# The first factor of a block inverse: from a product with the identity to a transposition on VectorE, with new weights and ranks for the list scheduler

## The reference

```
def step(state, inp):
    q_t, k_t, v_t, b_t, d_t = inp
    Sk = einsum('bhi,bhipj->bhpj', k_t, state)
    delta = (v_t - Sk) * b_t[..., None]
    state = state * d_t + einsum('bhi,bhpj->bhipj', k_t, delta)
    o = einsum('bhi,bhipj->bhpj', q_t, state)
```

## Time and profile before

| | |
|---|---|
| median of 3 runs | 1397.1 us (1396.12 to 1402.0) |
| span of the profiled execution | 1418.7 us; the profile gives no time beside it |
| TensorE busy | 1338.4 us, 94% |
| VectorE busy | 1126.6 us, 79% |
| ScalarE busy | 949.1 us, 67% |
| GpSimd busy | 698.8 us, 49% |
| the 64 rounds | about 350 to 1400 us of the span |

### The profile page before, as it was taken

One profiled execution on the slowest core, in us unless ns is written; L12 is line 12 of the kernel. 1 busy time (PEld: TensorE's weight loads), 2 busy tenths in 40 slices (PEclk: granted clock), 3 DMA queues, 4 the chain that ended last, 5 costly groups with the idle time before them and its releaser, 6 DMA issues.

```text
span 1418.7 us, 32580 instructions
## 1 busy us (share of the span) xinstructions
PE 1338.4 (94%) x12308; PEld 1091.0 (77%) x12308; DVE 1126.6 (79%) x2294; ACT 949.1 (67%) x2607; POOL 698.8 (49%) x806
## 2 busy tenths in 40 slices
PE   6999999778999999999999999999999998999997
PEld 3544446667888879888889798888888987789896
DVE  4587436889979788969798879697888897988886
ACT  3105751476777768777778678677687777787774
POOL 8012222337754565464745655556555557555431
PEclk9979999889999999999999999999999999999999
DMA  9900001212101121131311311312212114111000
GB/s 320 191 5 1 4 1 45 75 40 72 44 25 37 31 87 35 31 88 33 85 37 32 91 31 39 83 30 76 46 32 68 43 31 116 38 31 31 24 2 31
DMA packets 59507, 76.68 MB, mean 54 GB/s; under 512 B 6200, under 2 KB 46776, under 8 KB 59352
## 3 DMA queue, kind: packets, MB, share of 16 engines
q1 hardware_dynamic: 54616, 60.31, 16.7%
q0 software_dynamic: 4736, 14.29, 3.6%
HBM read 62.92 MB, written 11.67 MB: 53 GB/s over the span
## 4 chain that ended last, share of the span: by engine, by line
PE 60%; DVE 20%; ACT 6%; issue 5%; DMA 4%; POOL 3%; another core or an unknown queue 1%; SPq 0%; POOLq 0%; DVEq 0%; ACTq 0%
PE ps L930 10%; PE ps L1313 6%; DVE yv L1644 4%; PE ps L977 4%; DMA RC<-crow 3%; PE ps L1218 3%; DVE yk L1644 3%; PE ps L1266 2%; PE ps L1295 2%; PE ps L1228 2%; PE ps L1231 2%; PE ps L985 2%; PE ps L1282 2%; PE ps L1267 2%; PE ps L1291 2%
## 5 line engine op out<-in xcount | busy, mean ns | idle before, releaser
L1988 ACT ACTIVATE XY<-ps 128x512 f16<-128x512 f32 x384 | 221.2, 598 | 88.6 <-PE ps L1231 75.2
L1734 DVE TENSOR_TENSOR ZL<-ps,cst 128x256 f16<-128x256 f32 x384 | 155.0, 418 | 47.4 <-PE ps L1218 40.8
L1644 DVE SCALAR_TENSOR_TENSOR yv<-ps,cw,yv 128x511 f32<-128x511 f32 (+2 forms) x192 | 143.3, 746 | 7.0 <-ACT yv L1925 2.3
L930 PE MATMUL ps<-XH,WVh 128*128 128x256 f32 (+1 forms) x384 | 133.9, 349 | 1.2 <-ACT hT L1973 1.2
L1313 PE MATMUL ps<-WO,OGT 128*128 128x256 f32 x512 | 126.8, 391 | 3.2 <-DVE OGT L1806 2.9
L930 PE MATMUL ps<-XH,WVl 128*128 128x256 f32 (+1 forms) x384 | 123.5, 322 | 0.0
L930 PE MATMUL ps<-XL,WVh 128*128 128x256 f32 (+1 forms) x384 | 123.3, 321 | 0.0
L2181 POOL TENSOR_TENSOR RC<-RC,dec 128x512 f32<-128x512 f32 x64 | 69.3, 1083 | 100.8 <-DMA RC<-crow 100.6
L1228 PE MATMUL ps<-ZL,XY 128*128 128x64 f16 x1536 | 105.7, 193 | 8.1 <-DVE ZL L1734 4.4
L1218 PE MATMUL ps<-XY,LT 128*128 128x64 f16 x1536 | 101.1, 193 | 12.9 <-ACT XY L1988 11.1
L1218 PEld LDWEIGHTS ps<-XY,LT 128*128 128x128 f16 x1536 | 80.0, 98 | 42.4 <-issue 20.1
(11 more groups left out here) (305 smaller groups left out, 4122.0 us busy)
## 6 DMA issues: line engine op xcount, KB each, us to landing
RC<-crow SPq DMA_DIRECT2D x128, 128.0 KB
WV<-in_WV SPq DMA_DIRECT2D x16, 512.0 KB, 3.6
WK<-in_WK SPq DMA_DIRECT2D x16, 256.0 KB, 2.7
WO<-in_WO SPq DMA_DIRECT2D x16, 256.0 KB, 2.8
rows_out<-st SPq DMA_DIRECT2D x7, 512.0 KB
KS<-spread SPq DMA_DIRECT2D x12, 256.0 KB, 12.1
QS<-spread SPq DMA_DIRECT2D x12, 256.0 KB, 16.5
w<-in_w SPq DMA_DIRECT2D x4, 512.0 KB, 8.7
```

The source lines that it names most:

```text
L930: m = pe.matmul(o, a, b, start=c + k == 0, stop=c == 1 and k == 2)
L1644: m = dve.scalar_tensor_tensor(out=dst[:, k:512], in0=ps[:, bk, 0:512 - k], scalar=cw[:, h, j, 3 - k:4 - k], in1=dst[:, k:512], op0=ALU.mu ...
L1734: leave(dve.tensor_tensor(half(ZL[:, k - 2], k, 0), p, lv(k), ALU.mult), "a", u, k)
L1988: leave(act.activation(changed(u, k), ps[:, bank("b", u, k), :].rearrange("p (c n t) -> p c n t", c=2, t=1 << (k - 1)), ACT.Copy), "b", u, k)
```

## The change

TensorE's part of `x1` is removed, with the f16 identity that it used and the bank it took. VectorE's part becomes a transposition of 32x32 blocks from the second half of XY into the first, and it waits for `py` in place of the matmul; TensorE's `a` of level 2 waits for it on a semaphore of its own.

```diff
-    P.add(("x1", u), rank + 0.4, ("PE", 0.22, (("pl", u), "POOL"), (("cc", 1), "POOL")), ("DVE", 0.6, earlier(3, "r", "PE")), takes=True,
-          gives=("x1", u))
+    P.add(("x1", u), rank + 0.4, ("DVE", 0.6, (("py", u), "POOL"), earlier(3, "r", "PE")))
...
-                elif what == "x1":
-                    u = x[1]
-                    bk = enter(*x)
-                    w.wait_ge(s_const, 2)
-                    w.wait_ge(s_lt, nth("POOL", "pl", u))
-                    for l in range(4):
-                        m = pe.matmul(ps[:, bk, 128 * l:128 * l + 128], LT[:, u % 3, l, :], id16[:], start=True, stop=True)
-                    signal(m, *x)
                 elif what == "a":
...
-                        w.wait_ge(*done("x1", u))
+                        w.wait_ge(s_x, nth("DVE", "x1", u))
...
                 elif what == "x1":
                     u = x[1]
-                    w.wait_ge(*full(*x))
+                    w.wait_ge(s_y1, nth("POOL", "py", u))
                     if u > 2:
                         w.wait_ge(*full("r", u - 3))
-                    leave(dve.tensor_tensor(xy(u, 0), q4(bank(*x)), spread4(cst[:, C_X1:C_X1 + 128]), ALU.mult), *x)
+                    dve.transpose(XY[:, u % 3, 0, :], XY[:, u % 3, 1, :]).then_inc(s_x, 1)
...
-                    pool.tensor_copy(id16[:], ident).then_inc(s_const, 1)
```

The scheduler's numbers change with it. All entries of RANK are new (they were within about 190 of zero and now reach 919), as are the grain, the delays and about twenty planned durations; no other operation gains or loses work. Some of them:

```diff
-    GRAIN = 0.09700
-    DELAY = {"PE": 0.22, "DVE": 0.18, "ACT": 0.24, "POOL": 0.19, "SP": 0.1, "DMA": 0.1}
+    GRAIN = 0.11147
+    DELAY = {"PE": 0.21, "DVE": 0.16, "ACT": 0.19, "POOL": 0.13, "SP": 0.1, "DMA": 0.1}
...
-        P.add(x, rank[k], ("PE", 1.48, (("fWK", h), "POOL"), *(ready(b) if h < 3 else ())), ("ACT", 0.58, to), ("DVE", 1.99),
+        P.add(x, rank[k], ("PE", 1.48, (("fWK", h), "POOL"), *(ready(b) if h < 3 else ())), ("ACT", 0.58, to), ("DVE", 2.22),
...
-    P.add(("fWV", h + 2), 4 * h, ("SP", 4.5, *values), ("POOL", 3.8))
+    P.add(("fWV", h + 2), 4 * h, ("SP", 4.5, *values), ("POOL", 3.45))
...
-    P.add(("dec", u), rank, ("POOL", 2.1, (("row", u), "SP"), (("pre", 4), "DVE")),
+    P.add(("dec", u), rank, ("POOL", 1.82, (("row", u), "SP"), (("pre", 4), "DVE")),
```

More of the change, by code:

```diff
@@ L64 @@
 RANK = {
[4 rows of a table removed]
[L69 to L74, removed]
@@ L91 @@
-    "su": {"ACT": -16.946, "PE": 8.309}, "sw": {"DMA": -100.52, "POOL": -124.214}, "sx": {"POOL": -65.71},
-    "tn": {"DVE": -40.39, "PE": -186.124}, "tn0": {"DVE": -59.954}, "top": {"ACT": -153.89, "DVE": -156.062},
[3 rows of a table removed]
[4 rows of a table added]
+    "cb": {"DMA": -829.553, "DVE": 217.294, "POOL": 127.032}, "cc": {"POOL": -27.155},
+    "ck": {"ACT": -33.615, "DVE": 201.582, "PE": -3.762}, "cnt": {"DVE": 234.756, "PE": -2.423},
+    "cq": {"ACT": -199.157, "DVE": 145.393, "PE": -1.377}, "crow": {"ACT": -361.373, "PE": -155.287, "SP": 710.067},
@@ new lines @@
+    "cum": {"PE": -409.722}, "cv": {"ACT": -23.969, "DVE": 200.036, "PE": -0.564},
+    "dec": {"ACT": 47.457, "POOL": 169.749}, "dn": {"DVE": -285.719, "PE": -524.037},
+    "exd": {"DVE": -670.792, "PE": -138.789}, "exg": {"ACT": 258.114, "PE": -4.662},
+    "exv": {"DVE": -103.16, "PE": 2.115}, "fWK": {"POOL": -738.126, "SP": -270.056},
+    "fWO": {"POOL": 310.591, "SP": -213.119}, "fWV": {"POOL": -225.858, "SP": 145.206},
+    "fin": {"DVE": -248.233, "SP": -364.851}, "fs": {"ACT": -616.036}, "fup": {"POOL": -79.713, "SP": -72.817},
@@ new lines @@
+    "ot": {"DVE": 41.168, "PE": -104.679}, "ov": {"DVE": -329.735, "PE": -455.142},
+    "p1": {"DVE": -102.75, "PE": -219.755}, "pl": {"POOL": -567.038}, "pre": {"ACT": -424.57, "DVE": -587.097},
[4 rows of a table added]
+    "so": {"DVE": -370.925, "PE": -118.374}, "spg": {"POOL": 737.284}, "sq": {"ACT": 368.446, "POOL": 361.3},
+    "sr": {"DMA": 205.9, "POOL": 678.359}, "ss": {"SP": -866.232}, "stack": {"SP": 77.663},
+    "su": {"ACT": -114.55, "PE": -22.798}, "sw": {"DMA": -307.522, "POOL": 78.638},
+    "tn": {"DVE": -167.215, "PE": -172.959}, "tn0": {"DVE": -70.548}, "top": {"ACT": 383.052, "DVE": -352.188},
[3 rows of a table added]
@@ L186, in plan_experts0 @@
         x, y = ("exg", e, b), ("exv", e, b)
-        P.add(x, rank, ("PE", 1.81), ("ACT", 0.62, *old), takes=True, gives=x)
+        P.add(x, rank, ("PE", 1.81), ("ACT", 0.49, *old), takes=True, gives=x)
         P.add(y, rank + 1, ("PE", 1.81), ("DVE", 0.6, (x, "ACT")), takes=True, gives=y)
@@ L207, in plan_softmax0 @@
               ("DVE", 0.7, *[(("p1", b, g, i), "DVE") for g in range(8) for i in range(4)], (("tn0", 0), "DVE") if b else None))
-        P.add(("tn", b), -200 + 20 * b, ("PE", 0.44, (("tn0", b), "DVE")), ("DVE", 0.6), takes=True, gives=("tn", b))
+        P.add(("tn", b), -200 + 20 * b, ("PE", 0.46, (("tn0", b), "DVE")), ("DVE", 0.6), takes=True, gives=("tn", b))
         P.add(("max", b), -200 + 20 * b, ("SP", 5.0, (("tn", b), "DVE")))
@@ L231, in plan_rows0 @@
         b = n // 4
-        P.add(("op", n), -90 + 60 * b, ("PE", 1.72, *[(("am", b, g), "POOL") for g in range(4)]),
+        P.add(("op", n), -90 + 60 * b, ("PE", 1.8, *[(("am", b, g), "POOL") for g in range(4)]),
               ("DVE", 1.2, (("g0", b), "ACT"), (("op", n - 1), "DVE") if n else None), takes=True, gives=("op", n))
@@ L266, in plan_prologue @@
         P.add(("gt", b), -9, ("PE", 1.48, *ready(b), (("spg",), "POOL")), ("ACT", 0.6), takes=True, gives=("gt", b))
-        P.add(("gg", b), -9, ("PE", 0.44, (("gt", b), "ACT")), ("DVE", 0.45), takes=True, gives=("gg", b))
+        P.add(("gg", b), -9, ("PE", 0.46, (("gt", b), "ACT")), ("DVE", 0.45), takes=True, gives=("gg", b))
     both = [(("gg", b), "DVE") for b in range(2)]
@@ L272, in plan_prologue @@
     P.add(("pre", 3), -9, ("ACT", 1.7, (("pre", 2), "DVE")), ("DVE", 0.9))
-    P.add(("cum",), -9, ("PE", 1.0, (("pre", 3), "DVE")), takes=True)
-    P.add(("crow",), -9, ("PE", 0.44, (("pre", 3), "DVE")), ("ACT", 0.5), ("SP", 2.5), takes=True)
+    P.add(("cum",), -9, ("PE", 1.7, (("pre", 3), "DVE")), takes=True)
+    P.add(("crow",), -9, ("PE", 0.85, (("pre", 3), "DVE")), ("ACT", 0.5), ("SP", 2.5), takes=True)
     P.parts[("crow",), "ACT"].gives = ("crow",)
@@ L307, in plan_values @@
         x = "cv", h, v, b
-        P.add(x, rank[k], ("PE", 1.48, wv, *(ready(b) if h < 2 else ())), ("ACT", 0.58, (("Vt", h - 1, b, 1), "PE") if h else None), ("DVE", 1.99),
+        P.add(x, rank[k], ("PE", 1.48, wv, *(ready(b) if h < 2 else ())), ("ACT", 0.58, (("Vt", h - 1, b, 1), "PE") if h else None), ("DVE", 2.22),
               takes=True, gives=x)
@@ L402, in plan_routed @@
 def plan_routed(P):
-    P.add(("cnt",), -3.5, ("PE", 3.5, (("top", 2), "DVE")), ("DVE", 11.0, (("xr", 1), "SP")), takes=True, gives=("cnt",))
+    P.add(("cnt",), -3.5, ("PE", 6.0, (("top", 2), "DVE")), ("DVE", 11.7, (("xr", 1), "SP")), takes=True, gives=("cnt",))
     P.add(("slot",), -3.5, ("PE", 1.2, (("cnt",), "DVE")), ("DVE", 0.2), takes=True, gives=("slot",))
```

48 lines of the change are left out of this document (20 added, 28 removed), and 22 rows, old and new, of the table RANK.

## The result

The changed kernel is slower: 1408.4 us in the median of six runs (1404.6 to 1409.3) against 1398.6 for the kernel before (1396.1 to 1402.0), a ratio of 1.0063 with a 95% interval of 1.0050 to 1.0076. That is 9.8 us more, where 17 us less were forecast.

What follows compares the result with a forecast made beforehand. TensorE was taken as nearly full (97% busy in the rounds), VectorE often just behind. From the 1397.1 us median, 12.7 for slots and 4 for the list were subtracted, op and wait at nothing: 1380 us, own range 1372 to 1389, overall 1358 to 1398.

Steps and rivals of the forecast that it cites:

- the list: New order of all six queues: a gain of 4 us from two truer durations, bounds 17 us to either side.
- The slots: TensorE's queue loses the identity products, 64 x 0.22 = 14.1 us; nine tenths counted as time, 12.7 us.
- the wait: VectorE's first factor now waits for GpSimd's second: late in 16 of 64 rounds, 21.7 us together, charged nothing.
- hidden: Rival: VectorE or a DMA ends the waits, so only 60% of 14.1 us, 8.5, counts; 1393 us, chance 0.16.
- The op: VectorE's transposition in SBUF replaces a 682 ns multiplication from PSUM: taken as 0.68 us, nothing gained or lost.
- VectorE stands: Rival: GpSimd's second factor is late behind a DMA wait and VectorE's queue stands at the transposition; 1406 us, chance 0.10.
- its threshold of 117 us: In rival "VectorE stands", stalls added to VectorE's busy 883.6 us must take 117 us to exceed TensorE's 1001 us.
- the sign for right: In the rounds TensorE's idle time stays near 35 us, while its busy time falls by 14 to 25 us.
- the one for wrong: TensorE's idle time grows by the 14 us of queue that the removed products freed.

Runs made afterwards that it cites:

- the old order: The change put into before's written queues, only the product's entry removed, transposition at the multiplication's old place; 1415.4 against 1400.0 us, 1.0108.
- the second profile of before: The kernel before, unchanged, run and profiled again beside the experiments; 1402.2 us beside 1399.8, span 1400.5 us.
- last experiment, the mixed one: Before's order with product and bank kept in 26 rounds and the transposition in the other 38; 1395.96 against 1397.26 us, 0.9984.
- the old numbers and the new entry: Before's durations, grain, delays and ranks, planned anew with the transposition as its own entry and no bank; 1406.2 us, 1.0042 against before.
- 0.105 and 0.090: The kernel before, product kept, planned anew with the scheduler's GRAIN at these values instead of 0.097; 1.0033 and 1.0098 against before.
- the new front: Scheduler led through the changed kernel's 526 first decisions, then before's numbers, with the transposition; 1415.4 us, 1.0106 against before.
- the first profile: The kernel before, unchanged, profiled ahead of the prediction; span 1418.7 us.

## Why the prediction was wrong

The step that failed first is the list: the prediction took "a gain of 4 us" for giving up an order, and the runs show that with the product the order of before beats each of the three others that were planned, by 0.3 to 1.9%. The slots were sized at more than twice their worth, and the wait was put at nothing. Term by term:

- **The slots, nine tenths of 14.1 us.** The size of the queue was right (TensorE's busy time fell by 13.4 us from the second profile of before to the changed kernel), its worth was not: 0.4 to 0.6 in the order of before, so about 6 us of the 12.7, and next to nothing beside the stalls of the old order. What a slot is worth in the new order was not measured. The prediction had argued from TensorE's 97% that a slot must be time. The rows that spoke against it were its own, 60% of the chain, and it had used them for the rival "hidden" alone, whose 8.5 us was the nearer figure.
- **The op, 0.68 us.** Right: 702 ns, and VectorE's busy time is level. Two pages of the Trainium skill were weighed. "Vector Engine (DVE) Microarchitecture Reference", section "The reshape front-end and per-opcode configuration" (one element per cycle per lane), left the op near its old time, as the trace has it. The 1244 ns estimated in proportion to the figure of "VectorE: DVE Perf Modes", section "The three transpose paths", did not come.
- **The wait, nothing.** Its size in the rows was right to a microsecond for the old order, its price wrong. The step that failed here is "left where it is, the wait would put 21.7 us into VectorE's 166": room summed over the whole stretch does not cover a stall, since behind the stall stands a queue whose next op TensorE wants now. In the old order 22.6 us of stalls cost about 17 us (last experiment), and added alone 25.0 cost 14 us in the profiled executions and 21 in the medians. The mechanism there is that of the rival "VectorE stands", a DMA wait ahead of GpSimd's op and VectorE's queue behind it; only its threshold of 117 us was never needed. In the changed kernel the list keeps the stalls to 8.0 us, mostly by putting the transposition later, and VectorE's share of the chain is 10%. That the rival's 1406 us lies near the measured 1408.4 is therefore luck: its 140 us of stalls did not come. What the 8.0 us cost in the changed kernel was not measured.
- **The list, 4 us won.** This term has the wrong sign and is the one that was mis-sized most. With the old numbers and the new entry the waits are 2.6 us, yet the kernel is 5.9 us slower than before; if 6 us of slots were won there too, planning anew has lost some 12. That is an estimate of what is left over, not a measurement; that other orders lose is shown apart from it, by the product's own at 0.105 and 0.090 (0.33% and 0.98%). The new numbers add 0.2%, 3 us, of which the two intervals (1.0027 to 1.0056, 1.0050 to 1.0076) make little that is certain; the new front cost 9 us with the old rounds, and nothing that can be measured with the new ones. Truer durations for two kinds of op told nothing about the order.

The gap between forecast and result is 26 us, and by these estimates about 7 are from the slots, 12 from planning anew with what its stalls cost, 3 from the new numbers, and 4 the gain that was expected of them. The sum also took over 21.6 us between span and median from a profile that was probably of a slower chip. That the span of 1402 us forecast from it lies near the changed kernel's 1406.7 is no hit, since before's own second span is 1400.5; the forecast of the time doesn't depend on it. The bounds of the list term, 17 us to either side, were stated and then not carried into the range, which ended at 1398.

Of the signs named, the op lay in 0.6 to 0.8 us and the waits stayed below 20 us, both as for the forecast. Busy time fell by 17.6 us against the profile that the sign was written for, but by 13.4, just below its 14, against the second. TensorE's idle time from 350 to 1400 us is 37.7 us: level with the first profile's 34.6, and 8 us above the 29.4 of the second. That lies between the sign for right (near 35) and the one for wrong (14 more), and it is read over rounds that began 13 us later. The signs could not tell the result; the time did.

**What stays open.** Why before's order is better than its neighbours was not traced to operations. Nor is it known how much of a late front the rounds give back: in one pair they gave back nothing, in another all of it as far as can be measured. And no run has the changed kernel's order with its 8.0 us of stalls taken out.

## What to carry to other kernels

An operation moved to an input that comes later must be priced by what stands behind it in its engine's queue at each late round, not by that engine's idle total; set the starts side by side, and use the new form only in the rounds that have room. A freed slot on an engine that is 97% busy was worth here about what a doubled slot cost, 0.4 and 0.6 of its length, and doubling is easily measured first, on the old order; beside new stalls it was worth almost nothing. And where an order is planned by numbers chosen for one graph, any change of the graph is compared with a fitted order by an unfitted one: move a number a little on both sides before crediting or blaming the change.

## What the runs showed of the hardware

**A short stall of TensorE can halve its clock inside a busy stretch.** In the kernel with the change in the old order TensorE stands 2.66 us for VectorE's C, which stands behind a transposition that waits 2.77 us. First its timeline, then the stretches around:

```profile
1190.68 0.61 PE L1250 MATMUL ps<-C,R 128*128 128x128 f16 x4 [2.66 <-DVE C L1740]
```

```profile
1190.00:1195.00 5.00, 4.32 (x24) 3.97 (x25) 4.54 (x10) 1.06 (x1) 4.08 (x6) 0.50 0.09 26
1195.00:1200.00 5.00, 5.00 (x44) 4.34 (x43) 4.33 (x11) 3.16 (x11) 3.19 (x4) 0.82 0.28 82
```

and the first of the two in the second profile of before:

```profile
1190.00:1195.00 5.00, 4.49 (x39) 3.65 (x38) 4.83 (x13) 3.21 (x13) 3.59 (x4) 1.00 0.29 82
```

The granted clock is 0.50, the 1.2 GHz level, over the 5 us that begin with the stall's last 0.7 us, and 24 matmuls are counted there where 39 were, though of other work, since this kernel is some 5 us behind. Before's second profile has no piece of 5 us below 0.95 in the rounds up to 1390 us; the kernels with added waits have one or two such stretches each. It doesn't follow on every stall: in the same kernel TensorE stands 1.93 us at 1293 us, and in the mixed one 2.24 us at 1185 us, with no such piece after them. Nor is it the waits' alone, since the first profile of before has two such stretches (0.76 from 900 and 0.66 from 990 to 995 us). A stall that is followed by one costs more than its length, by little here: in the kernel with the wait alone the clock is 0.95 and 0.71 in two pieces of 5 us, 1.7 us of clock in all. The Trainium skill, page "TensorE: Matmul & The Clock Gate", section "What's actually happening", says that the default is throttled and activity releases it; the fall in a stall of 2.66 us agrees with that.

**A VectorE op with both inputs in SBUF can take three times its time while GpSimd works**: 683 ns in the median, 960 in the mean, 2416 at most, for the multiplication of LT by a mask, with both inputs in SBUF. 27 of the 64 took over 720 ns, and a GpSimd op was running during each of the 27, for 85% of their time in the mean, against 43% for the other 37. GpSimd's work alone isn't enough, since nine of the 37 were covered to over 90% and stayed short. The longest ran beside GpSimd's own op on two SBUF inputs, ML from M and MHi, among others. The transposition, with one input in SBUF, never took over 712, though in the old order GpSimd was at work during over 90% of it in 33 of 64 rounds. The Trainium skill, "GPSIMD Engine Reference", section "1. Specifications", has GpSimd's SBUF interfaces in contention with VectorE instructions of two SBUF inputs. The trace agrees.

**Chips differ.** The kernel before took 1397 to 1400 us in the median on the other chips and 1417 on one.
